# Attention block on one core: raw x transposed against centred projection weights, row deviations put into V and its sums column

## What is computed

```python
def _layernorm(x, eps=1e-05):
    return (x - mean(x)) / sqrt(var(x) + eps)

def attention(x):                         # x is already layer-normed
    qkv = (x @ w_qkv).reshape(1, 2048, 16, 24)
    q, k, v = split(qkv, 3)               # per head: 8 numbers each
    w = relu(q @ k.T / sqrt(8))
    attn = w / (sum(w) + 1e-06)
    y = x + (attn @ v) @ w_out + b_out
    return (y - mean(y)) * rsqrt(var(y) + 1e-05) * gamma + beta

def ffn(x):
    return sqrt((x @ cos(theta + theta_noise))**2 + (x @ sin(phi + phi_noise))**2)

x = x + attention(_layernorm(x))
x = x + ffn(_layernorm(x))
```

## Time and profile before

| | us |
|---|---|
| median of 3 runs (431.34 to 431.54) | 431.46 |
| the profiled execution | 431.37 |
| its span in the trace | 429.6 |
| PE busy | 417.0 (97%) |
| ACT busy | 340.4 (79%) |
| DVE busy | 330.8 (77%) |
| POOL busy | 46.0 (11%) |

### The profile page before, as it was taken

How to read it: one execution, slowest core, us unless ns; L and a number is a source line. 1 busy time by engine, 2 the same in 40 slices (tenths; PEclk the granted TensorE clock), 3 DMA queues, 4 the chain that set the end, 5 groups by cost and what they waited for, 6 DMA issues and landing times.

```text
span 429.6 us, 9007 instructions
## 1 busy us (share of the span) xinstructions
PE 417.0 (97%) x3294; PEld 123.3 (29%) x3294; DVE 330.8 (77%) x656; ACT 340.4 (79%) x595; POOL 46.0 (11%) x57
## 2 busy tenths in 40 slices
PE   7899999999999999999999999999999999999985
PEld 5333222222222332222222332222222332222244
DVE  6775788777688877777778877777778876777857
ACT  2767878788788878888888878888888878888843
POOL 4794000000001001000001011000001011000101
PEclk9999999999999999999999999999999999999999
DMA  5027841001021100201011100201011000101100
GB/s 165 25 50 148 166 105 50 2 14 36 2 57 50 42 10 2 73 2 50 2 55 51 31 22 2 73 2 51 2 52 54 2 27 0 50 2 33 35 2 26
DMA packets 11134, 17.42 MB, mean 41 GB/s; under 512 B 3092, under 2 KB 4756, under 8 KB 10708
## 3 DMA queue, kind: packets, MB, share of 16 engines
q1 hardware_dynamic: 10948, 16.70, 14.5%
q10 hardware_dynamic: 144, 0.13, 0.2%
HBM read 3.86 MB, written 5.10 MB: 21 GB/s over the span
## 4 chain that ended last, share of the span: by engine, by line
PE 92%; DVE 3%; ACT 3%; issue 1%; DMA 1%; POOL 0%; DVEq 0%
PE pv L993 58%; PE sc L960 27%; PE pv L1046 1%; ACT w_buf L535 1%; PE pv L892 1%; PE pv L901 1%; PE pv L913 1%; DMA x_sb<-x_dram 1%; PE pv L1019 1%; ACT w_buf L532 0%; PE pv L1000 0%; DVE stats L639 0%; DVE x L781 0%; PE sc L1046 0%; PE sc L1000 0%
## 5 line engine op out<-in xcount | busy, mean ns | idle before, releaser
L993 PE MATMUL pv<-w_buf,v_sb 128*32 128x512 f32 x2048 | 272.3, 604 | 0.0
L685 DVE TENSOR_SCALAR w_buf<-sc 128x512 f32<-128x512 f32 x256 | 176.7, 690 | 78.7 <-PE sc L960 70.8
L532 ACT ACTIVATE w_buf<-sc 128x512 f32<-128x512 f32 x256 | 153.3, 599 | 68.6 <-PE sc L960 67.8
L535 ACT ACTIVATE w_buf<-sc 128x512 f32<-128x512 f32 (+1 forms) x256 | 184.9, 722 | 0.0
L960 PE MATMUL sc<-q_rep,k_rep 32*128 32x512 f32 x1024 | 136.2, 493 | 2.8 <-ACT w_buf L535 1.2
L689 DVE TENSOR_SCALAR w_buf<-sc 128x512 f32<-128x512 f32 x179 | 121.8, 680 | 1.3 <-PE sc L960 1.3
L960 PEld LDWEIGHTS sc<-q_rep,k_rep 32*128 32x128 f32 x1024 | 53.1, 181 | 218.6 <-ACT w_buf L532 175.9
L993 PEld LDWEIGHTS pv<-w_buf,v_sb 128*32 128x32 f32 x2048 | 40.4, 108 | 66.6 <-ACT w_buf L535 35.2
L450 POOL TENSOR_TENSOR oT<-o_raw,o_scale 128x512 f32<-128x512 f32 (+1 forms) x4 | 5.1, 1281 | 267.9 <-issue 167.4
L921 PE MATMUL pv<-ident 128*128 128x128 f32 x64 | 9.1, 310 | 1.5 <-POOL ident L391 1.5
L456 POOL TENSOR_TENSOR x<-x,mv 128x512 f32<-128x512 f32 (+1 forms) x5 | 4.4, 886 | 47.3 <-DVE x L781 47.3
(11 more groups left out here) (104 smaller groups left out, 136.2 us busy)
## 6 DMA issues: line engine op xcount, KB each, us to landing
pv_dram<-pv_sb SPq DMA_DIRECT2D x15, 256.0 KB, 2.0
q_rep<-q_hi SPq DMA_DIRECT2D x30, 64.0 KB, 2.1
q_rep<-q_lo SPq DMA_DIRECT2D x30, 64.0 KB, 2.1
k_rep<-k_hi SPq DMA_DIRECT2D x6, 256.0 KB, 4.1
k_rep<-k_lo SPq DMA_DIRECT2D x6, 256.0 KB, 5.4
x_sb<-x_dram SPq DMA_DIRECT2D x3, 256.0 KB, 3.9
o_raw<-pv_dram SPq DMA_DIRECT2D x3, 256.0 KB
o_scale<-inverse_dram SPq DMA_DIRECT2D x3, 256.0 KB
```

The source lines that it names most:

```text
L532: nc.scalar.activation(w_buf[:, s % W_STEPS, 0, :], early[:, 0, :], ACT.Relu).then_inc(relu[0], 1)
L535: nc.scalar.activation(w_buf[:, s % W_STEPS, 2:2 + n, :], late[:, 0:n, :], ACT.Relu).then_inc(relu[0], 1)
L685: nc.vector.tensor_scalar(w_buf[:, s % W_STEPS, 1, :], early[:, 1, :], 0.0, None, ALU.max).then_inc(relu[1], 2 if both else 1)
L993: last = nc.tensor.matmul(bank[32 * i:32 * i + 32, :], v_sb[:, k, HPG * g + i, :], w_buf[:, s % W_STEPS, i, :], start=(k == 0), stop=(k == ...
```

## The change

**The projections.** Layer normalisation of a row is (x - mean) * r, with r = 1/sqrt(var + eps). The centring is taken into the weights: POOL forms `centring` = identity - 1/128, and one matmul on PE multiplies w_qkv with it (into a half of sc[2]). PE transposes the raw x as it is loaded. The factor r of a query row cancels between weights and their sum; only the guard, 1e-6 * sqrt(8), has to be multiplied with the row's deviation 1/r. The factor r of a key row is put into V: ACT's `take_v` writes V times r squared (`inv_var`, four instructions with a scale for each tile instead of one copy) and r itself into the sums column (one root instruction of 64 columns).

**Moved.** DVE no longer normalises chunk 0, but takes the centred weights from PSUM into w_rep and w3 (`take_weights`), which POOL did before from SBUF. `statistics` is cut into `statistics` and `variance`, and both of chunks 2 and 3 are hooks of pass 0. The roots of the variances are taken behind steps (0, 12) and (0, 13). POOL pads groups 1 to 3 in one go once the first keys and queries are there (`rep_ready`), waits for the four roots, forms `eps_std` (guard times deviation), writes it to DRAM (2048 single numbers), normalises all four chunks (chunk 0 with them), loads the guards back in the layout of the sums (`eps_spread`, four transfers) and then does the subtractions and additions for which it was free before. The ones in V's sums column are gone. Chunk 0 of x is one transfer of 256 KB from ACT's queue, w_qkv is the first from SP's. `transpose_x(1)` and `take_xT(1)` stand ahead of the first projections. `warm_up` has 8 matmuls instead of 12, and ACT takes both late results at step (0, 4) instead of (0, 1).

```diff
@@ POOL, start of the kernel @@
+                nc.gpsimd.memset(averager[:, :], 1 / D).then_inc(averager_ready, 1)
...
+                nc.gpsimd.tensor_tensor(centring[:, :], ident[:, :], averager[:, :],
+                                        ALU.subtract).then_inc(centring_ready, 1)
...
                     nc.gpsimd.memset(v_sb[:, :, heads, HD + 1:VW], 0.0).then_inc(v_pad, 1)
-                    nc.gpsimd.memset(v_sb[:, :, heads, HD:HD + 1], 1.0).then_inc(v_pad, 1)
...
-                normalise_x(1)
-                normalise_x(2)
-                pad_v(1)
-                normalise_x(3)
-                for g in range(2, G):
+                pool.wait_ge(rep_ready, 2)
+                for g in range(1, G):
                     pad_v(g)
-                nc.gpsimd.memset(averager[:, :], 1 / D).then_inc(averager_ready, 1)
+                pool.wait_ge(rstd_ready, NC)
+                nc.gpsimd.tensor_tensor(eps_std[:, :], var_eps[:, :], rstd[:, :], ALU.mult).then_inc(std_ready, 1)
...
+                pool.dma_start(eps_dram.rearrange("t p -> p t"), eps_std[:, :], allow_slow_non_contiguous=True).then_inc(eps_saved, 16)
+                for c in range(NC):
+                    normalise_x(c)
+                pool.wait_ge(eps_saved, 16)
+                for c in range(NC):
+                    pool.dma_start(eps_spread[:, c, :], eps_dram[chunk(c), :].rearrange("t (u b) -> (t u) b", u=2)
+                                   .unsqueeze(0).to_broadcast([H, HD, H * CW // P])).then_inc(eps_loaded, 16)
@@ ACT @@
-                    nc.scalar.copy(v_sb[:, chunk(c), :, 0:HD],
-                                   v_bank[c].rearrange("p (t h d) -> p t h d", t=TPC, h=H)).then_inc(v_ready, 1)
+                    act.wait_ge(var_ready, c + 1)
+                    nc.scalar.activation(v_sb[:, chunk(c), :, HD],
+                                         inv_var[:, chunk(c)].unsqueeze(2).to_broadcast([P, TPC, H]), ACT.Sqrt)
+                    for t in range(TPC):
+                        n = c * TPC + t
+                        last = nc.scalar.activation(v_sb[:, n, :, 0:HD],
+                                                    v_bank[c][:, t * P:(t + 1) * P].rearrange("p (h d) -> p h d", h=H),
+                                                    ACT.Copy, scale=inv_var[:, n:n + 1])
+                    last.then_inc(v_ready, 1)
...
-                act.dma_start(x_sb[:, 2:TPC, :], x_v[:, 2:TPC, :]).then_inc(x_second, 16)
-                root(0)
+                act.dma_start(x_sb[:, 0:TPC, :], x_v[:, 0:TPC, :]).then_inc(x_loaded[0], 16)
...
+                             ((0, 12), lambda: root(0)), ((0, 12), lambda: root(1)),
+                             ((0, 13), lambda: root(2)), ((0, 13), lambda: root(3)),
@@ DVE @@
+                def take_weights():
...
+                    dve.wait_ge(w_centred, 1)
+                    for n in (1, 0):
+                        nc.vector.tensor_copy(w_rep[:, n, :].rearrange("p (h d j) -> p h d j", h=HPG, j=4),
+                                              centred_w[:, n, 0:HPG].unsqueeze(3).to_broadcast([P, HPG, HD, 4])
+                                              ).then_inc(w_rep_ready, 1)
+                    nc.vector.tensor_copy(w3[:, :, :].rearrange("p c (h d) -> p c h d", h=H),
+                                          centred_w).then_inc(w3_ready, 1)
...
-                    own(nc.vector.tensor_scalar_add(sums[rows, :], sums[rows, :], DEN_EPS))
+                    dve.wait_ge(eps_loaded, 16 * NC)
+                    own(nc.vector.tensor_tensor(sums[rows, :], sums[rows, :], eps_spread[rows, c, :], ALU.add))
@@ PE @@
-                    pe.wait_ge(xn_ready, c)
+                    pe.wait_ge(x_loaded[c], 16)
...
+                nc.tensor.matmul(sc[2][:, 1, 0:3 * D], centring[:, :], wqkv_sb[:, :], start=True,
+                                 stop=True).then_inc(w_centred, 1)
+                transpose_x(1)
```

92 lines of the change are left out of this document (51 added, 41 removed).

## The result

The changed kernel takes **445.25 us** (median of 4 runs, 444.57 to 445.65), the kernel before 431.48 us beside it (4 runs, 431.34 to 431.54). The ratio is 1.0318, 95% interval 1.0302 to 1.0334: 13.8 us slower. The forecast was 433.6 with 436.5 as its upper end. The sign was right, and so was the place; the size was wrong by a factor of six.

A forecast was written before the change was run, and what follows sets the result against it. PE bounds the kernel, busy 97% of the span, so other engines count only where PE waits for them. 431.37 less 1.5 for the start-up plus 3.7 lost in pass 0 gave 433.6 us, range 429.6 to 436.5.

The forecast's parts named there:

- The step that failed: Pass 0, DVE's angles beside POOL's bias work: each wait lasts only for POOL's running instruction, 0.6 us on average.
- Its two events, L781 and L632: Kernel's end and start-up: two DVE instructions, 701 ns and 1.02 us, read as waiting for POOL's running instruction.
- 4.5 - 0.76 = 3.7 forecast: Pass 0: 4.5 us of DVE waits less 0.76 of DVE's idle time, so PE loses 3.7 us.
- seven small ones: Pass 0: waits at seven steps of angles, 0.6 us each, plus two of 1.1: 6.4 us at full overlap.
- four issues: Pass 0: POOL's issuing of four transfers, a reason to take 0.7 of 6.4 us, so 4.5.
- The guard's transfer of 2048 single numbers: Pass 0: some 10 us taken, between 3.5 to 3.9 and 62; without any wait the additions start at 57.9.
- rival 1: Pass 0: the guard's transfer lands late, POOL is idle during DVE's angles, only the start-up's gain stays: 429.9 us; chance 0.32.
- What would have shown it: Signs: POOL's additions beside DVE's angles, angle instructions of 0.8 to 1.6 us, PE's scores there up to 1.5.
- The start-up: Up to step (0, 2): first scores at about 10.3, the second half of its scores at 14.5 instead of 16.03; 1.5 us gained.
- rival 3: Start-up: slow PE rows after the shorter warm-up, no gain; 434 to 436 with POOL's loss, 430.9 without; no separate chance.
- `take_v(0)`: Start-up, ACT: one copy becomes a root of 0.21 us and four scaled instructions of 0.295 each, 1.4 us.
- L666's wait: Start-up, in DVE's variance(1): waits beside POOL's first padding, about 1 us instead of 0.17, so 0.85 added.

The follow-up runs named there:

- e2: The kernel before, with POOL's bias work made to wait for the scores of step 25, so that it runs beside DVE's angles: 436.83 us.
- e7: The kernel before, with POOL's bias work made to wait for the scores of step 26, beside DVE's angles: 436.23 us.
- e9: The kernel before, bias work waiting for the scores of step 25, with four transfers issued by POOL directly ahead of its subtractions: 446.58 us.
- e13: The kernel before, bias work beside DVE's angles, with one transfer issued by POOL directly ahead of its subtractions: 444.39 us.
- e4: The changed kernel without POOL's eight additions; the four subtractions stay: 434.88 us.
- e10: The changed kernel with one real wait of POOL, for the end of its memset of o_sb, between that memset and the subtractions: 436.10 us.
- e3: The changed kernel with each of POOL's twelve bias instructions but the first waiting for the one before it to complete: 436.46 us.
- e12: The changed kernel with the four transfers that spread the guard issued by SP's queue instead of POOL's: 436.27 us.
- e5: The changed kernel with its first angle instruction as a SCALAR_TENSOR_TENSOR with factor 1.0 instead of a TENSOR_TENSOR: 445.64 us.
- e1: The changed kernel with POOL's subtractions and additions waiting until DVE's last angle instruction is done: 430.81 us.
- e11: The changed kernel with POOL's bias work behind DVE's angles and its three paddings of V waiting for variance(1): 430.63 us.
- e8: The changed kernel with POOL's bias work ahead of the four transfers that spread the guard, instead of behind them: 437.28 us.

## Why the prediction was wrong

- **The step that failed**: "In both DVE waited for POOL's running instruction and then took its normal time", and from it "the first of a step meets POOL anywhere in an instruction of 1.0 to 1.24 us, so 0.6 on average". Its two events, L781 and L632, stood behind no transfer of POOL's, as the kernel before has none. The rule holds there, and by e2 and e7 it is right: of 5.0 us between the marks in e2 3.4 are waits, against 4.5 - 0.76 = 3.7 forecast. It doesn't hold in a row that POOL starts directly behind a transfer of its own (e9, e13), and the change puts four of them directly ahead of the row. The wait was 12.0 us (12.42 less its own 0.41), once, and not seven small ones.
- **The prediction named the four issues but made them an argument for less overlap** ("since POOL also issues four transfers in this stretch"). The row directly behind them held DVE off for 12.0 us, where the sum had 4.5 for all waits.
- **The clock was missing from the sum.** Of the 14.39 us between the marks 2.5 are PE at its lower level behind the gap; in e2 the clock has 1.6, and in e4 1.6 us came behind a gap of 2.30. Waits that stop PE cost more than their length here, also where no gap is as long as 2 us: e2's was 1.94, e10's 1.73, e3's 1.59 and e12's 0.83, and the clock fell to 0.50 behind each. The prediction had the clock only in the start-up.
- **What was right**: POOL's bias work lies beside the angles. The guard's transfer of 2048 single numbers took 12.5 us from issue to landing (some 10 taken), so that the bias work started at 58.3 and its additions at 62.3 instead of 57.9; POOL was then far from idle when DVE came, so that rival 1 didn't decide. The Trainium skill, DMA: Bandwidth & Descriptors, section "Rules for kernel authors", has one descriptor for each element of such a transfer; the time is in line with it, but doesn't prove it: 8 KB took 12.5 us, and 256 KB in long pieces 3.9 or, from SP's queue in the same stretch, 5.0. What the trace counts are packets, and this transfer has 48 (all of POOL's queue in e12).
- **What would have shown it** was worded too narrowly: "the angles' instructions should take 0.8 to 1.6 us" fits e2, e3 and e10. In the changed kernel one took 12.42 and nine were as before.
- **The start-up gave 0.52 us by the mark instead of 1.5.** The first scores came at 11.41, not 10.3: x landed at 5.24 (4.6), and PE, whose warm-up ran until then, started the transposes at 5.27 (4.9). From start to start the transposes took 0.91 us (0.66) and the centring matmul 1.18 (0.68), which were sized from rows at PE's full pace. That is the mechanism of rival 3; with the 0.37 us of the late start it makes the 1.1 us. In e5's execution, with fast rows, step (0, 2) was at 14.53, where 14.5 was forecast, and the mark was 1.30 early.
- **Right in the start-up**: `take_v(0)` (1.4 us forecast, 1.29 taken, 10.88 to 12.17), next to no cost of the roots (at most 0.2 us, with `take_v`, by the first mark), and L666's wait, 1.08 for 1.02:

```profile
11.69 1.08 DVE L666 TENSOR_SCALAR var_eps<-mv 128x4 f32<-128x4 f32 x1
```

All told, the change without the loss (e1) is worth 0.45 us in the median, and with the padding moved too (e11) 0.7 (its interval and e1's overlap), where the prediction had 1.5 for the start-up.

## What to carry to other kernels

Beside DVE's work on SBUF, don't let GpSimd start a row of instructions directly behind a transfer that it has issued: issue the transfer from another queue or behind the row, or make GpSimd wait once for something that it has just done. Best is to keep the two engines' work apart: e1 was 5 us faster than the best kernel with short waits (430.81 against 436.10). Before an instruction of such a row is moved, look at what DVE does at its new place, and price the wait by the length of the whole row, not of one instruction. And where waits stop TensorE, look for the clock behind the gap and add it: it was 1.6 us behind gaps of 1.94 (e2) and 2.30 (e4), and 2.5 behind 11.80.

## What was not expected of the hardware

- In a row that GpSimd started directly behind a transfer that it had issued, one or four, DVE's next instruction with all operands in SBUF was held off to the end of the row: 12.42, 12.62, 13.02, 13.18 and 11.57 us in five kernels with rows of twelve, for three forms of instruction, and 2.93 with a row of four. Without the transfer, or with one pause of 0.14 us behind it, the longest took 1.4 to 1.5 us. Instructions of DVE that read PSUM kept their 0.68 to 0.69 us beside the rows. The runs show when it happens and not how it comes about.
- The Trainium skill, SBUF — State Buffer, section "SBUF: two separate sides", warns of the opposite case, in which DVE keeps GpSimd from preparing a transfer; no run here shows that one.
- The pace of such a row differs a little: the additions start 1.22 us apart in the changed kernel, in e9 and in e13, and 1.24 on average in the kernel before. It is a hint at most, as single distances of 1.22 stand in e8 and e12 too.
- TensorE was granted its lower level behind gaps of 2.30 (e4), 1.94 (e2), 1.73 (e10) and 1.59 us (e3), in e12 with no gap over 0.83, and in one execution (e1) at 14 us with none over 0.6 ahead of it. What decides it stays open.
